# Last stage of an audio tower: the router's small rows in PSUM, its logits between the first two expert tiles

## The reference, cut to what matters

```
logits  = x.mean(axis=1) @ router_w.T            # one row of 11 per sequence
probs   = softmax(logits)
top 2 of probs, divided by their sum
weights = sum over the two of value * pw[index]  # six expert weights per sequence
h_e     = gelu(x @ W1[e] + b1[e])                # 128 -> 341, for all six experts
out     = sum over e of weights[e] * (h_e @ W2[e] + b2[e])
h       = h + out
```

## Time and profile before

| what | value |
|---|---|
| median of 3 runs | 835.07 us (834.08 to 836.67) |
| span of the profiled execution | 837.2 us |
| mean granted TensorE clock of the core | 0.875 |
| PE, DVE, ACT, POOL busy, share of the span | 76%, 75%, 63%, 34% |

### The profile page before, as it was taken

One profiled execution on the slowest core, in us unless ns is written; L12 is line 12 of the kernel. 1 busy time (PEld: TensorE's weight loads), 2 busy tenths in 40 slices (PEclk: granted clock), 3 DMA queues, 4 the chain that ended last, 5 costly groups with the idle time before them and its releaser, 6 DMA issues.

```text
span 837.2 us, 11023 instructions
## 1 busy us (share of the span) xinstructions
PE 635.0 (76%) x3178; PEld 489.5 (58%) x3179; DVE 631.0 (75%) x1271; ACT 524.3 (63%) x837; POOL 281.6 (34%) x313
## 2 busy tenths in 40 slices
PE   6998652653717355389767899988899999999998
PEld 4554652653717355275545589844667667667665
DVE  1786597999999999997874312167798898997853
ACT  1588999999899898982232134352575565575452
POOL 0465000000010000000377244416356666664552
PEclk9998876967769586789666799999999999999999
DMA  5380044344445554441411366320000000000000
GB/s 182 121 303 20 1 85 72 72 86 86 80 76 103 100 104 79 72 72 60 163 30 33 92 179 179 100 69 0 1 1 10 1 10 8 3 11 6 5 10 19
DMA packets 26384, 56.52 MB, mean 68 GB/s; under 512 B 4203, under 2 KB 15572, under 8 KB 25860
## 3 DMA queue, kind: packets, MB, share of 16 engines
q0 software_dynamic: 5728, 24.56, 15.6%
q1 hardware_dynamic: 19848, 30.80, 12.2%
q10 hardware_dynamic: 764, 0.62, 0.2%
HBM read 29.91 MB, written 10.17 MB: 48 GB/s over the span
## 4 chain that ended last, share of the span: by engine, by line
PE 39%; DVE 28%; issue 15%; ACT 11%; DMA 3%; SPq 2%; POOL 2%; another core or an unknown queue 1%; DVEq 0%; ACTq 0%; POOLq 0%
PE psum L2035 5%; DVE s_R L1265 3%; DVE s_R L1252 3%; PE psum L1749 3%; DVE s_R L1276 2%; PE psum L1951 2%; PE psum L2022 2%; PE psum L1959 2%; PE psum L1821 2%; PE psum L1822 2%; PE psum L1823 2%; PE psum L2091 2%; PE psum L2023 2%; PE psum L2024 2%; PE psum L2068 2%
## 5 line engine op out<-in xcount | busy, mean ns | idle before, releaser
L1821 PE MATMUL psum<-s_xn_lo,s_split_hi 128*128 128x368 f32 x256 | 95.0, 371 | 137.6 <-ACT s_R L911 134.8
L1821 PEld LDWEIGHTS psum<-s_xn_lo,s_split_hi 128*128 128x128 f32 x256 | 54.7, 214 | 142.3 <-ACT s_R L911 137.5
L671 POOL DMA_DIRECT2D s_xnfm<-s_R x14 | 17.1, 1219 | 257.3 <-DVE s_R L1276 257.3
L1271 DVE TENSOR_TENSOR_SCAN s_R<-s_R 128x2944 f32<-128x2944 f32 x16 | 100.7, 6292 | 0.8
L1047 ACT ACTIVATE s_R<-psum,s_cols 128x368 f32<-128x368 f32 x96 | 49.5, 566 | 70.2 <-PE psum L2024 70.1
L1822 PE MATMUL psum<-s_xn_hi,s_split_lo 128*128 128x368 f32 x256 | 92.1, 360 | 0.0
L1823 PE MATMUL psum<-s_xn_hi,s_split_hi 128*128 128x368 f32 x256 | 91.6, 358 | 0.0
L2035 PE MATMUL psum<-s_R 128*128 128x368 f32 x256 | 90.1, 478 | 0.0
L767 POOL TENSOR_TENSOR s_R<-s_R 128x368 f32<-128x368 f32 x48 | 46.7, 974 | 61.8 <-DVE s_R L1676 60.0
L730 POOL TENSOR_TENSOR s_R<-s_R 128x368 f32<-128x368 f32 x47 | 54.2, 1154 | 38.1 <-DVE s_R L1546 20.0
L918 ACT ACTIVATE s_R<-psum,s_cols 128x736 f32<-128x736 f32 x64 | 56.1, 876 | 14.0 <-PE psum L1823 10.1
(11 more groups left out here) (256 smaller groups left out, 1654.7 us busy)
## 6 DMA issues: line engine op xcount, KB each, us to landing
s_xnfm<-s_R POOLq DMA_DIRECT2D x14, 1472.0 KB, 10.5
s_R<-in_w SPq DMA_DIRECT2D x28, 256.0 KB
s_R<-in_xg SPq DMA_DIRECT2D x7, 744.0 KB, 4.1
x_sorted<-in_x_init SPq DMA_DIRECT2D x1, 5082.0 KB
s_wBC<-in_wBC SPq DMA_DIRECT2D x8, 256.0 KB, 2.8
s_R<-in_v SPq DMA_DIRECT2D x2, 1024.0 KB
s_R<-x_sorted SPq DMA_DIRECT2D x28, 66.0 KB
s_R<-in_w SPq DMA_DIRECT2D x1, 1536.0 KB, 6.8
```

Of the source, the lines that this page charges most:

```text
L1271: dve.tensor_tensor_scan(bufB[:, u], ra[:, u], bufB[:, u], 0.0, ALU.mult, ALU.add).then_inc(ra_free, 1)
L1821: pe.matmul(bank(c), w_hi[:, s, u, k, :], xn_lo[:, a:b], start=True, stop=False)
```

## The change

Four edits in the last stage:

- The router's small rows `z` lie in the first 128 columns of bank 5, on four partitions, instead of SBUF. One row, `zz[2]`, keeps a place in SBUF (`z_one`), since it is read together with another of the rows. The columns `zs` and the rows from `ewp` on stay in SBUF.
- ScalarE copies bank 5 once (`stream_hi`, into `xn_hi`), and signals `nF.xT_free` behind that. The copy into `xnfm` is gone; VectorE's split and sums read bank 5.
- `expert_weights` multiplies straight from PSUM, and the copy into `ew` comes behind it without a wait between them.
- TensorE's logits are issued between the first and the second expert tile of the chunk, in the passes with attention.

```diff
--- before.py
+++ after.py
@@ -469,7 +469,8 @@
         ftmp = take(2, CT)
         fo = take(2, CB, D, parts=L)
         srep = take(CB)
-        z = take(8, 16, parts=CB)
+        z = psum[0:CB, 5, 0:8 * 16].rearrange("p (k n) -> p k n", k=8)
+        z_one = take(16, parts=CB)
         zs = take(8, parts=CB)
         euler = take(1, parts=CB)
         bias_added = sem("bias_added")
@@ -1084,6 +1085,10 @@
                                          scale=rstd[:, u, j:j + 1], bias=nmr[:, u, j:j + 1])
                 ins.then_inc(nF.xs_ready, 1)
 
+            def stream_hi(f):
+                act.wait_ge(nF.xT_ready, 2 + f + 1)
+                act.activation(fm(xn_hi, f % 2), bank(5), ACT.Copy).then_inc(nF.xT_free, 1)
+
             def shares_out(c):
                 act.wait_ge(PT_ready, c + 1)
                 act.activation(P_hi[:, c % 2], bank(3, OH), ACT.Copy).then_inc(P_hi_ready, 1)
@@ -1106,7 +1111,7 @@
                 if c < NCH:
                     shares_out(c)
                 if 1 <= c <= NCH:
-                    norm_copies(act, nF, (c - 1) % 2, c - 1, (5, 5), dst=xnfm, hi=xn_hi)
+                    stream_hi(c - 1)
                 if c >= NCH:
                     rest_out(c - 2)
                 gelus(c - 1, 0, 6)
@@ -1515,7 +1520,7 @@
                 yield both_ends(o3, 0, E1, 1), both_ends(q3, 0, E1, 1), both_ends(k3, o, L - K, 0)
 
             N = slice(0, NPART)
-            zz = [z[:, k, N] for k in range(8)]
+            zz = [(z_one if k == 2 else z[:, k])[:, N] for k in range(8)]
             s1 = [zs[:, k:k + 1] for k in range(8)]
 
             def ts(o, a, x, y, p, q=None):
@@ -1613,11 +1618,11 @@
 
             def split_stream(c):
                 dve.wait_ge(nF.xT_free, c + 3)
-                dve.tensor_tensor(fm(xn_lo, c % 2), fm(xnfm, c), fm(xn_hi, c % 2).bitcast(f32), ALU.subtract)\
+                dve.tensor_tensor(fm(xn_lo, c % 2), bank(5), fm(xn_hi, c % 2).bitcast(f32), ALU.subtract)\
                     .then_inc(xf_split, 1)
 
             def stream_sums(c):
-                dve.tensor_reduce(srep, fm(xnfm, c).rearrange("p (b l) -> p b l", b=CB), AX, ALU.add)\
+                dve.tensor_reduce(srep, bank(5).rearrange("p (b l) -> p b l", b=CB), AX, ALU.add)\
                     .then_inc(srep_ready, 1)
 
             def shares_rest(c):
@@ -1658,11 +1663,11 @@
 
             def expert_weights(f):
                 dve.wait_ge(ew_mm, f + 1)
-                step.add(dve.tensor_copy(ew, psum[:, 5, 464:464 + NE * CB].rearrange("p (e b) -> p e b", e=NE)))
-                step.wait()
+                spread = psum[:, 5, 464:464 + NE * CB].rearrange("p (e b) -> p e b", e=NE)
                 step.add(dve.tensor_tensor(
                     wrt, rmask.rearrange("p r (o e) -> p r o e", o=1).to_broadcast([D, NR, CB, NE]),
-                    ew.rearrange("p e (o b) -> p o b e", o=1).to_broadcast([D, NR, CB, NE]), ALU.mult))
+                    spread.rearrange("p e (o b) -> p o b e", o=1).to_broadcast([D, NR, CB, NE]), ALU.mult))
+                step.add(dve.tensor_copy(ew, spread))
                 step.wait()
                 dve.tensor_reduce(wr, wrt, AX, ALU.add).then_inc(ew_ready, 1)
                 dve.wait_ge(ew_ready, f + 1)
@@ -2177,7 +2182,12 @@
                     elif 1 <= o <= 3:
                         if o == 1:
                             ffn(f - 1, 28, 30)
-                        ffn(f, 2 * o - 2, 2 * o)
+                            ffn(f, 0, 1)
+                            if tail:
+                                router_logits(f)
+                            ffn(f, 1, 2)
+                        else:
+                            ffn(f, 2 * o - 2, 2 * o)
                     elif o == 4:
                         ffn(f - 1, 30, NF)
                     elif o == 5:
@@ -2186,7 +2196,7 @@
                         if tail:
                             router_spread(f)
                         ffn(f, 8, 12)
-                    if o == 1 and tail:
+                    if o == 1 and tail and not att:
                         router_logits(f)
                 if c + 1 < NCH:
                     pe.wait_ge(pb_free, c * K + K - 1)
```

## The result

The changed kernel took 830.12 us (median, 829.34 to 830.84, 4 runs), the kernel before 834.58 us (833.16 to 836.67, 4 runs): a ratio of 0.9943, 95% interval 0.9925 to 0.9961, faster by more than the 0.3% that can be told. Timed again beside the experiments it had 0.9949 (0.9931 to 0.9968). The forecast was 831.3 us and a gain of 3.8 us; the medians give 4.5. One of the twelve executions of experiment 4 took 1572 us, for a reason that nothing here shows, and is left out of its ratio.

The account below looks back on a forecast made before the run. TensorE was taken as the last stage's bound, busy 28.11 of 30 us. 6 x 0.50 + 0.8 = 3.8 us off 835.07 gave 831.3 us; own range 829.6 to 833.3, eight in ten 829.5 to 834.0.

Parts of the forecast that it names:

- The stall: TensorE's wait before L2133 for the router's weights: 0.50 us in each of six chunks, 1.16 us in chunk 1.
- The cause: VectorE's small router operations wait for GpSimd's adds; PSUM rows free L1523 (minus 1.00 us) and L1368 (minus 0.61 us).
- The chain: Offset 4 starts when TensorE delivers, near 726.0; 2.16 us later L1656 could release L2133, at 728.16.
- The collision of the 4x6 operation: The 4x6 L1523, still in SBUF, moves into GpSimd's add and ends later; 0.1 us comes back.
- In hand: Slack before L2133 once its stall is closed: weights possible at 728.16, TensorE free at 729.06, 0.9 us.
- PSUM's price: Extra cost of small router operations on PSUM rows: taken as none, upper bound 0.15 us more for each of five.
- Rival 1: PSUM rows are dear in the router: 831.6 us, or 832.1 if chunk 1 gives nothing; chance 0.12.
- Split, copy, expert weights at nothing: Split 0.2 us shorter, ScalarE's dropped copy and the expert product from PSUM: all worth 0 on TensorE's path.
- Logits: L2128 between the two expert tiles: sums ready at 721.47, TensorE there at 721.8, cover 0.3 us, no wait.
- Given back at the next wait: Before the softmax, time won could be lost to a GpSimd hold-up; VectorE's 0.77 us wait is the cover.
- Rival 2: GpSimd holds up the attention's products (L1585), the wait for L1612 grows, 3.0 us lost: about 834.3 us; chance 0.12.
- rival 4: VectorE's small router rows stay blocked by GpSimd even in PSUM; the stalls stay, 835 us; chance 0.06.

Follow-up runs that it names:

- experiment 4: The changed kernel with the router's small rows back in SBUF, the other edits kept; ratio 0.9984 to the kernel before.
- Experiments 5 and 6: Kernel before with only the 4x66 product's row in PSUM, 0.9967; changed kernel with only that row back in SBUF, 0.9953; both ratios to the kernel before.
- experiment 1: The kernel before with only the router's small rows moved to PSUM; ratio 0.9966 to the kernel before.
- experiment 8: The changed kernel with ten unread 4x11 reduces added to the router's weights; 838.83 us, ratio 1.0050 to the kernel before.
- Experiment 3: The kernel before with only ScalarE's single copy and VectorE's split and sums read from bank 5; ratio 0.9989 to the kernel before.

## Why the prediction was right, by its own steps

- **The stall.** 0.50 us in six chunks was to go wholly, and did (distance 0.75 to 0.25). In chunk 1 the gain was to be 0.8, and the distance fell by 0.79: the record of offset 4 ends at 595.01 + 0.33 = 595.34 and L2138 starts 2.21 us later, where 2.16 us behind VectorE's start were forecast.
- **The cause.** That VectorE's small operations wait for GpSimd's adds, and don't with a row in PSUM, held for both operations: 1.22 to 0.22 and 0.81 to 0.19. The Trainium skill, "SBUF — State Buffer", section "Who interferes with whom", names the two cases (two SBUF inputs, which contend with GpSimd's reads, and tensor_scalar, which can contend). Experiments 5 and 6 agree with it for each separately, experiment 1 for both. One reading was incomplete: the 1.22 us were not the add's alone, the exponential in front of it held the operation first.
- **The chain.** Offset 4 was to start when TensorE delivers, 0.0 us behind its record; it starts 0.09 behind (718.59 + 0.33 = 718.92, and 719.01). L1533 was put at 0.16 us and took 0.21; it didn't matter, since VectorE still waited 0.29 us for offset 4. From there to a possible L2138 2.16 us were forecast; L1661 ends 2.06 us behind the offset's start, and with the handover of 0.06 that makes 2.12. The collision of the 4x6 operation came, at 0.07 us instead of 0.1. In hand were to be 0.9 us; it was 0.93 by the trace and 0.88 by experiment 8.
- **PSUM's price.** None was assumed. The results in PSUM cost 9 ns on the tensor_scalar, and seven operations in a row 0.03 us. The Trainium skill, "Perfetto Trace Analysis", section "Optimizing Scalar/DVE Operations", gives an overhead of about 60 ns for SBUF and 125 ns for PSUM. By an estimate from these figures each such operation would be 65 ns dearer, and no row shows that. Rival 1 is refuted.
- **Split, copy, expert weights at nothing.** Experiment 3 agrees for split and copy: 31.70 against 31.74 us per chunk. The expert weights were not tried alone; experiment 1, which lacks that edit, has the whole change's 31.23 us.
- **Logits.** TensorE doesn't wait: the sums end at 713.81 + 0.53 = 714.34, L2133 starts at 714.82. The cover is 0.5 us, more than the 0.3 forecast.
- **Given back at the next wait.** VectorE waits 1.02 us instead of 0.77 before expert 2: it only runs further ahead. The wait for L1617 stayed at 5.3 us. Rival 2 is refuted; rival 4 too.
- **The size.** 6 x 0.51 and 0.55 us in chunk 1 (counted between the same events of the two traces, 551.76 to 603.04 and 546.82 to 597.55) make 3.6 us; the spans from the first transposes to the end differ by 3.5. The forecast said 3.8. The medians' 4.5 and 4.1 us have intervals of some 1.5 us to either side, so the last 0.5 us or so can't be told from scatter. One thing was left out, the clock around chunk 1. The stretches with the low clock, before, after, and the same place in the second trace of the changed kernel (columns as in the earlier trace rows, the clock is the third number from the end):

```profile
580.45:583.85 3.40, 3.25 (x13) 0.85 (x10) 3.33 (x12) 0.11 (x1) 3.16 (x4) 0.50 0.00 0
594.10:597.50 3.40, 3.40 (x13) 2.95 (x13) 1.95 (x9) 1.14 (x2) 0.97 (x1) 0.50 0.00 0
```

```profile
586.75:593.55 6.80, 6.27 (x21) 5.33 (x21) 3.76 (x15) 1.71 (x3) 1.99 (x3) 0.50 0.01 2
```

```profile
586.00:597.00 11.00, 8.72 (x47) 6.74 (x47) 7.69 (x33) 5.27 (x11) 4.39 (x5) 1.00 0.01 1
```

The granted clock was 0.50, the lower level of 1.2 GHz, for 6.8 us both before and after, but before in two halves, one of them ahead of chunk 1's router. In the second trace of the changed kernel it didn't fall at all. The waits of TensorE just ahead were the same in both traces of the changed kernel (0.45 us for L1617, 0.77 and 0.76 us for L1630), so these waits alone don't decide whether it falls; what does isn't shown. Its price is 2.24 us: from the first transposes of the stage to L2138 of chunk 1 the changed kernel took 50.73 us with the fall and 48.49 without. That is more than half of the whole gain, between two executions of one kernel. For the same reason the 0.55 us of chunk 1 compares two different placements of the low clock. Experiment 3's kernel has its 6.8 us within a microsecond of the place where the changed kernel has them, and its router stalls much as before (1.29 us); it took 51.60 us over that distance, 0.87 us more than the changed kernel. So the 0.8 us forecast for chunk 1 is borne out where the clock is alike.

## What to carry to other kernels

When a tiny VectorE operation shows a time many times that of its twin, look at what GpSimd runs under it, and give the operation a PSUM operand: here one row of 4x11 was worth as much as the whole edit in chunks 2 to 7. Price such a fix by the stall it closes (0.50 us) and not by the busy time it removes (1.8 us per chunk in the three operations): what lies beyond the stall becomes slack. And measure slack by adding work until it shows: ten dummy operations gave 0.88 us where the trace gave 0.93, or 0.87 without the handover of 0.06. And before crediting a gain of a few us, compare the granted clock of the two traces stretch by stretch: here one fall more or less was worth 2.24 us.

## What the runs showed of the hardware

- A VectorE operation that has to wait for GpSimd can sit through two GpSimd instructions in a row. In experiment 4 the 4x11 operation starts at 720.38 under GpSimd's exponential (719.93 to 720.48). It isn't let in between that and the add that starts at 720.46 (the two records leave no gap), and ends 0.03 us behind the add. So a block can be longer than any one GpSimd instruction: 1.22 us in the earlier trace rows, with an exponential of 0.55 and adds of 0.96.
- Small VectorE operations cost almost the same with their rows in PSUM as in SBUF: 157 against 153 ns for the 4x11 reduce, 225 against 216 ns for a tensor_scalar that writes PSUM instead of SBUF, 1.48 against 1.45 us for seven operations in a row.
- The granted clock can fall to 0.50 for 6.8 us in one execution of a kernel and stay at 1.00 in the next, behind the same waits of TensorE. In the fall the matmuls of 368 columns started 0.31 us apart (at 590.30 and 590.61 in the first trace), without it 0.17 (at 591.06 and 591.23 in the second).
